# GpSimd sums half of the first layer's normalisation and mixes two tiles, and the key and value stores end in the next stage

## The reference, cut to what matters

```python
xn = layernorm(x)
# layer 0, attention: one head of width 128
q, k, v = split(xn @ Wqkv + bqkv);  a0 = softmax(q @ k.T * scale) @ v @ Wo + bo
# layer 0, second branch: 4 streams of 128 columns; 16 + 4 + 4 logits a row from the rms-normed xn
K = exp(H_res_logits / 0.1)                  # 4x4 for each row of x
for _ in range(50): row = 1 / (K @ col);  col = 1 / (K.T @ row)     # Sinkhorn, 100 halves
H_res = (1 - g) * I + g * row * K * col      # g = sigmoid(gate)
y = (streams weighted by H_pre) @ W_branch
f0 = H_res @ streams + H_post x y
x = x + a0 + f0
xn = layernorm(x)
# layer 1, attention: 32 query heads, 8 key heads, causal, keys and values by way of latents of 32
q = xn @ Wq.T;  k = (xn @ Wk_down.T) @ Wk_up.T;  v = (xn @ Wv_down.T) @ Wv_up.T
a1 = softmax(mask(q @ k.T * scale)) @ v @ Wo.T
# layer 1, second branch: one matrix product and 8 low-rank experts, 2 a row by a gate
f1 = xn @ weight.T + sum_e w_e * (xn @ A_e) @ B_e / 16
out = x + a1 + f1
```

## Time and profile before

| | |
|---|---|
| median of 3 runs | 2350.42 us (2345.44 to 2351.66) |
| the profiled execution | 2352.82 us, its span 2351.0 us |
| mean granted TensorE clock | 0.984 |
| PE, PEld busy | 2226.2 us (95%), 1810.6 us (77%) |
| DVE, ACT, POOL busy | 1536.4 us (65%), 1070.2 us (46%), 1014.8 us (43%) |

### The profile page before, as it was taken

One profiled execution on the slowest core, in us unless ns is written; L12 is line 12 of the kernel. 1 busy time (PEld: TensorE's weight loads), 2 busy tenths in 40 slices (PEclk: granted clock), 3 DMA queues, 4 the chain that ended last, 5 costly groups with the idle time before them and its releaser, 6 DMA issues. The chain is left out here.

```text
span 2351.0 us, 34663 instructions
## 1 busy us (share of the span) xinstructions
PE 2226.2 (95%) x11190; PEld 1810.6 (77%) x11190; DVE 1536.4 (65%) x3818; ACT 1070.2 (46%) x2279; POOL 1014.8 (43%) x1124
## 2 busy tenths in 40 slices
PE   6799897999999999999998888999999999999998
PEld 5554676888888888878786767888888888888886
DVE  6777565777677777756565564656566666666665
ACT  2456233545554444445444232545454544444444
POOL 5331713444445453676764011525344444434341
PEclk9999998999999999999999999999999999999999
DMA  9600564010101010111100464010101010101000
GB/s 349 207 0 10 213 234 156 10 63 9 63 9 63 14 58 27 45 47 42 44 28 6 173 245 157 28 48 24 62 9 62 9 62 9 62 9 62 27 32 32
DMA packets 74168, 165.26 MB, mean 70 GB/s; under 512 B 4721, under 2 KB 38897, under 8 KB 67442
## 3 DMA queue, kind: packets, MB, share of 16 engines
q1 hardware_dynamic: 73650, 162.95, 19.7%
q10 hardware_dynamic: 432, 1.32, 0.1%
HBM read 113.40 MB, written 72.61 MB: 79 GB/s over the span
## 5 line engine op out<-in xcount | busy, mean ns | idle before, releaser
L1852 DVE TENSOR_TENSOR pT<-psum,pT 128x512 fp32r<-128x512 f32 x576 | 387.1, 688 | 262.1 <-ACT pT L1900 259.8
L1752 POOL TENSOR_TENSOR probs_even<-probs_even,rinv 128x1024 f32<-128x1024 f32 (+2 forms) x192 | 241.0, 1255 | 553.9 <-DVE rinv L1843 553.9
L1900 ACT ACTIVATE pT<-psum 128x512 fp32r<-128x512 f32 x576 | 330.9, 596 | 317.8 <-PE psum L1961 317.7
L1838 DVE CUSTOM_DVE_ANT_0 psum<-psum,causal 128x256 f32<-128x256 f32 (+7 forms) x512 | 385.8, 766 | 37.3 <-PE psum L97 33.4
L1891 ACT ACTIVATE probs_even<-psum,nmax 128x1024 f32<-128x1024 f32 (+3 forms) x256 | 204.3, 798 | 247.2 <-DVE nmax L1838 243.4
L1752 POOL TENSOR_TENSOR probs_odd<-probs_odd,rinv 128x896 f32<-128x896 f32 (+2 forms) x192 | 198.9, 1043 | 257.5 <-DVE rinv L1843 257.3
L95 PE MATMUL psum<-keys,q 128*128 128x512 f32 (+3 forms) x768 | 265.7, 346 | 3.7 <-DVE q L1793 2.8
L97 PE MATMUL psum<-keys,q 128*128 128x512 f32 (+3 forms) x768 | 262.1, 341 | 0.0
L96 PE MATMUL psum<-keys,q 128*128 128x512 f32 (+3 forms) x768 | 262.0, 341 | 0.0
L95 PE MATMUL psum<-pT,vals 128*128 128x512 f32 x576 | 256.6, 445 | 4.3 <-DVE pT L1852 0.4
L1891 ACT ACTIVATE probs_odd<-psum,nmax 128x896 f32<-128x896 f32 (+3 forms) x256 | 176.4, 690 | 146.0 <-DVE nmax L1838 143.1
(11 more groups left out here) (304 smaller groups left out, 4423.5 us busy)
## 6 DMA issues: line engine op xcount, KB each, us to landing
k_parts<-kv_out SPq DMA_DIRECT2D x32, 512.0 KB, 4.7
wq<-wq_copy SPq DMA_DIRECT2D x16, 1024.0 KB, 4.8
v_parts<-kv_out SPq DMA_DIRECT2D x32, 512.0 KB, 3.6
wo<-wo_copy SPq DMA_DIRECT2D x16, 1024.0 KB, 4.8
keys<-k_parts SPq DMA_DIRECT2D x32, 512.0 KB, 4.5
vals<-v_parts SPq DMA_DIRECT2D x64, 256.0 KB, 3.1
acc<-in_x SPq DMA_DIRECT2D x4, 1024.0 KB, 12.0
xn_later<-xn SPq DMA_DIRECT2D x1, 2048.0 KB, 14.7
```

Source lines behind the costliest of these rows:

```text
L1752: pool.tensor_tensor(p, p, rinv[:, u, h:h + 1].to_broadcast([P, (TB - u) * P]), ALU.mult).then_inc(p_ok, 1)
L1838: dve.tensor_tensor_reduce(out=row, in0=row, in1=causal[:, S - n:S], scale=-1.0, scalar=-2 * MASKED, op0=ALU.add, op1=ALU.min, accum_out=n ...
L1852: dve.tensor_tensor(pT[:, n % PT_SLOTS, 1, :], bank[T_BANK + n % 2], f32(pT[:, n % PT_SLOTS, 0, :]), ALU.subtract).then_inc(t_lo, 1)
L1900: act.activation(pT[:, n % PT_SLOTS, 0, :], bank[T_BANK + n % 2], ACT.Copy).then_inc(t_hi, 1)
```

## The change

**Normalisation.** GpSimd, having scaled part 1 (`OWN`), also sums it by two additions: columns 2 and 3 onto 0 and 1 in place, then those two into `sk_s`. DVE sums part 0 alone and inverts both. The folding by logarithms stands at the stage's start, and the 68 halves run in one loop. The table of `between` has a maximum every 5 halves, 20 for a unit, and head sums at other places; the last unit's four head sums come after the mixing. **Attention of layer 0.** A unit's first scores are issued ahead of the head outputs of the unit before, the branch product stands between the second and third head output, and `share` takes one tile after each exponential. **Mixing.** DVE takes tiles 0 to 3, GpSimd 4 and 5 by `tensor_tensor` with broadcast weights (a product of 128x4x128 and an addition for each stream and for `y`), ScalarE and TensorE 6 and 7, with 8 slots at another place in memory and 4 of the 10 products issued within the last unit. GpSimd adds `bo` to tile 5 in `layer0_project`. **`layer1_inputs`.** With b = 0 too the main sums of tiles 6 and 7 stand after the `ups`; the weights' load and the spill or return stand ahead of the stores; the end of the stage no longer waits for the stores. That wait is in `layer1_attention`: SP's ahead of the keys, GpSimd's ahead of the mask. **`layer1_attention`.** Other `mixing_steps`.

```diff
+KV_SLOTS, UPS = 4, 32
...
-            add_bo(3)
-            add_bo(4)
+            for t in range(3, TB - 2):
+                add_bo(t)
...
-        FIRST_MAX, PER_UNIT = 3, 17
-        BY_ACT, SHARE_SLOTS = range(TB - 3, TB), UQ
-        CHUNKS = (SINKHORN_ITERS - SINKHORN_CHUNK - EARLY_HALVES // 2, SINKHORN_CHUNK)
+        FIRST_MAX, PER_UNIT, HALVES = 7, 20, 2 * SINKHORN_ITERS - EARLY_HALVES
+        BY_POOL, BY_ACT, SHARE_SLOTS = range(TB - 4, TB - 2), range(TB - 2, TB), 8
+        slots = placed(nc, "slots", XT, [P, SHARE_SLOTS, NS, D])
+        def out_bank(t):
+            return bank[(7, 6, 0, 1)[t % UQ] if t >= NT - UQ else 7 - t % 2][:]
...
-                with pool.Fori(0, count) as it:
-                    for half in range(2):
-                        for k in range(PARTS):
-                            factor = wide_rows(part_of(row, k)) if half else wide_cols(part_of(col, k))
-                            pool.wait_ge(factor_ok[k], it * 2 + (have + half))
-                            pool.tensor_tensor(part_of(T, k), part_of(K, k), factor, ALU.mult).then_inc(scaled[k], 1)
+            pool.wait_ge(k_ok, 1)
+            with pool.Fori(0, HALVES // 2) as it:
+                for half in range(2):
+                    for k in range(PARTS):
+                        factor = wide_rows(part_of(row, k)) if half else wide_cols(part_of(col, k))
+                        pool.wait_ge(factor_ok[k], it * 2 + (1 + half))
+                        pool.tensor_tensor(part_of(T, k), part_of(K, k), factor, ALU.mult).then_inc(scaled[k], 1)
+                    ours = turned_part(part_of(T, OWN)) if half else part_of(T, OWN)
+                    two = ours[:, :, :, 0:2]
+                    pool.wait_ge(scaled[OWN], it * 2 + (1 + half))
+                    pool.tensor_tensor(two, two, ours[:, :, :, 2:4], ALU.add).then_inc(halved, 1)
+                    pool.wait_ge(halved, it * 2 + (1 + half))
+                    pool.tensor_tensor(part_of(sm, OWN), two[:, :, :, 0], two[:, :, :, 1], ALU.add).then_inc(summed[OWN], 1)
+            pool.wait_ge(mix_ok, 1)
+            steps = 0
+            for t in BY_POOL:
+                x = x1[:, t, :].rearrange("p (i c) -> p i c", i=NS)
+                for j in range(NS + 1):
+                    stream = xn[:, t, j * D:(j + 1) * D] if j < NS else y[:, t, :]
+                    weight = T[:, t, :, j] if j < NS else rw[:, t, 1, :]
+                    if j == 0:
+                        pool.wait_ge(x1_ok, t + 1)
+                    if j == NS:
+                        pool.wait_ge(y_ok, t // UQ + 1)
+                    if steps:
+                        pool.wait_ge(blended, steps)
+                    pool.tensor_tensor(products[:], stream.unsqueeze(1).to_broadcast([P, NS, D]),
+                                       weight.unsqueeze(2).to_broadcast([P, NS, D]), ALU.mult).then_inc(blended, 1)
+                    pool.wait_ge(blended, steps + 1)
+                    pool.tensor_tensor(x, x, products[:], ALU.add).then_inc(blended, 1)
+                    steps += 2
...
-                dve.scalar_tensor_tensor(out=x1[:, t, :], in0=bank[7 - t % 2][:], scalar=rinv[:, t:t + 1], in1=x1[:, t, :],
+                dve.scalar_tensor_tensor(out=x1[:, t, :], in0=out_bank(t), scalar=rinv[:, t:t + 1], in1=x1[:, t, :],
                                          op0=ALU.mult, op1=ALU.add).then_inc(x1_ok, 1)
-            between = {0: [(weights_max, 0)], 2: [(weights, 0)], 5: [(gates, 0)], 9: [(later_head, 0)]}
-            for t in range(NT):
-                at = FIRST_MAX + PER_UNIT * (t // UQ)
-                k = t % UQ
-                between.setdefault(at + 4 * k, []).append((maximum, t))
-                between.setdefault(at + 4 * k + 3, []).append((invert, t))
-                between.setdefault(at + PER_UNIT + (14 if t // UQ < UNITS - 1 else 5) + k, []).append((add_heads, t))
+            between = {0: [(weights, 0)], 1: [(maximum, 2)], 3: [(maximum, 3)], 4: [(gates, 0)], 5: [(later_head, 0)],
+                       6: [(invert, t) for t in range(UQ)]}
+            for t in range(UQ, NT):
+                at = FIRST_MAX + PER_UNIT * (t // UQ - 1) + 5 * (t % UQ)
+                between.setdefault(at, []).append((maximum, t))
+                between.setdefault(min(at + 7, HALVES - 1), []).append((invert, t))
+            for t in range(NT - UQ):
+                between.setdefault(FIRST_MAX + PER_UNIT * (t // UQ + 1) + (1, 1, 3, 4)[t % UQ], []).append((add_heads, t))
+            weights_max(0)
+            dve.wait_ge(logs_ok, 2)
+            after(dve.tensor_tensor(Z[:], Z[:], wide_rows(lrow[:]), ALU.add))
+            dve.tensor_tensor(Z[:], Z[:], wide_cols(lcol[:]), ALU.add).then_inc(z_ok, 1)
             for k in range(PARTS):
-                dve.sem_inc(factor_ok[k], 1)
-            for part, count in enumerate(CHUNKS):
-                before = 2 * CHUNKS[0] * part
-                if part:
-                    dve.wait_ge(logs_ok, 2)
-                    after(dve.tensor_tensor(Z[:], Z[:], wide_rows(lrow[:]), ALU.add))
-                    dve.tensor_tensor(Z[:], Z[:], wide_cols(lcol[:]), ALU.add).then_inc(z_ok, 1)
-                    for k in range(PARTS):
-                        dve.memset(part_of(col, k), 1.0).then_inc(factor_ok[k], 1)
-                for half in range(before, before + 2 * count):
-                    for k in range(PARTS):
+                dve.memset(part_of(col, k), 1.0).then_inc(factor_ok[k], 1)
+            maximum(0)
+            maximum(1)
+            for half in range(HALVES):
+                for k in range(PARTS):
+                    if k != OWN:
                         by = turned_part(part_of(T, k)) if half % 2 else part_of(T, k)
                         dve.wait_ge(scaled[k], half + 1)
                         dve.tensor_reduce(part_of(sm, k), by, AX.X, ALU.add).then_inc(summed[k], 1)
-                        dve.wait_ge(summed[k], half + 1)
-                        dve.reciprocal(part_of(col if half % 2 else row, k), part_of(sm, k)).then_inc(factor_ok[k], 1)
-                    for step, t in between.pop(half, ()):
-                        step(t)
-                for k in range(PARTS):
-                    dve.wait_ge(factor_ok[k], before + part + 1 + 2 * count)
-                if part == 0:
-                    dve.sem_inc(factors, 1)
+                    dve.wait_ge(summed[k], half + 1)
+                    dve.reciprocal(part_of(col if half % 2 else row, k), part_of(sm, k)).then_inc(factor_ok[k], 1)
+                for step, t in between.pop(half, ()):
+                    step(t)
+            for k in range(PARTS):
+                dve.wait_ge(factor_ok[k], 1 + HALVES)
...
-            mixes, at = 0, 2 * sum(CHUNKS)
+            mixes, at = 0, HALVES
             ready = {t: (x1_ok, t + 1) for t in range(TB)}
-            for tiles in ((0, 1), (2, 3, 4)):
+            for tiles in ((0, 1), (2, 3)):
...
+            for t in range(NT - UQ, NT):
+                add_heads(t)
...
+            act.activation(lcol[:], col[:], ACT.Ln).then_inc(logs_ok, 1)
+            act.wait_ge(z_ok, 1)
+            act.activation(K[:], Z[:], ACT.Exp).then_inc(k_ok, 1)
+            act.wait_ge(chain, RW_MAX)
+            act.activation(rw[:], rw[:], ACT.Exp).then_inc(rw_exp, 1)
...
+            def share(t):
+                if t == 0:
+                    act.wait_ge(chain, RW_DONE)
+                if t >= UQ:
+                    act.wait_ge(xp_mm, t // UQ)
+                for j in range(NS):
+                    act.activation(shares[:, t % UQ, j, :], xn[:, t, j * D:(j + 1) * D], ACT.Copy,
+                                   scale=rw[:, t, 0, j:j + 1]).then_inc(xp_ok, 1)
...
+                    act.wait_ge(part_mm, e - SHARE_SLOTS + 1)
+                for i in range(NS):
+                    act.activation(slots[:, e % SHARE_SLOTS, i, :], xn[:, t, j * D:(j + 1) * D] if j < NS else y[:, t, :], ACT.Copy,
+                                   scale=T[:, t, i, j:j + 1] if j < NS else rw[:, t, 1, i:i + 1]).then_inc(part_ok, 1)
...
+                            if unit == UNITS and j % 2:
+                                product(j // 2)
...
-                        if t == 1:
-                            share(0)
-                        if t == 2:
+                        share(t)
+                        if t == UQ:
...
+                        if unit == 2:
+                            if qt == 0:
+                                act.wait_ge(m.ffn_in, 16 * 5)
+                            weight_high(wf_h[:, qt, :], wf_l[:, qt, :])
+                            if qt:
+                                high, low = m.right[0][qt - 1]
+                                weight_high(high[:], low[:])
...
-                if 0 < unit < UNITS:
-                    share(unit)
...
-            high, low = m.right[0][-1]
-            act.activation(high[:], f32(low[:]), ACT.Copy).then_inc(m.ffn_hi, 1)
+            for e in range(TB // 2, (NS + 1) * len(BY_ACT)):
```

(57 more changed lines are left out.)

79 lines of the change are left out of this document (17 added, 62 removed).

## The result

The changed kernel takes **2369.67 us** (median of 4 runs, 2369.08 to 2371.58) against 2350.43 us: 1.0079 times as long, with a 95% interval of 1.0064 to 1.0094. It is 19 us slower where 20 us less were forecast, and lies outside the range. The profiled execution has a span of 2367.3 us, 16.3 more than that of before.

A forecast was written before the change was run, and what follows sets the result against it. TensorE was taken to bound the attention stages, GpSimd and DVE's chain the normalisation, stores `layer1_inputs`. Terms +4 - 15 - 9 + 0 = -20 us from 2352.8 gave 2332.8, carried over to the median as 2330 us; range 2312 to 2346.

The forecast's parts named there:

- Mixing steps: First attention stage: GpSimd's steps move from units 5 and 6 to 2 and 7; net 0 us, between -6 and +7.
- The net of 0: Sum for the attention mixing steps: 7.7 us of `probs_even` waits gone, against 2.4 us delays in three iterations and 3.5 us key waits twice.
- GpSimd's sums: Second stage: GpSimd sums part 1, so a plain half takes 1.35 us, not 0.91; stretch to the weights 110.6 us, +3.
- DVE's wait of the earlier trace should go; I leave 2 us: Second stage: DVE's 8.3 us wait for scores goes with earlier scores and spread shares, leaving 2 us for units 2 and 3.
- Rival B: Second stage: GpSimd's sums are dear, 1.55 us a half, 13 us more, 2343 us; chance 0.14.
- Mixing: First layer, from the weights on: GpSimd's operations block DVE's steps; 46 us against 45.5, bounds 31 and 53.
- rival A: First-layer mixing: no blocking of DVE by GpSimd, tail 31 us, 15 us less, 2315 us; chance 0.18.
- `layer1_inputs`, b = 0: First half of the rows: earlier stores, loads ahead of them, no wait for the last landing; -15 us, bounds -8 and -17.
- Second half: Second input stage: loads ahead of stores give -6, half the bytes in the spill's return -3; -9 us, bounds -4 and -11.
- Rival C: Slower: a normalisation half costs 1.65 us and eats 20 us of gain; at 1.8 us the kernel takes 2360 us; chance 0.07.
- Rival D: Input stages: stores set everything anyway, so they give 5 + 3 us instead of 24; 2346 us; chance 0.09.

The follow-up runs named there:

- a2: The changed kernel, with SP issuing the third tile's loads behind those of keys, first values and output weights: 2352.7 us, ratio 1.0004.
- c1: The changed kernel, with ScalarE's copy of `oT` ahead of the last exponential of the next unit in the second stage: 2361.1 us, ratio 1.0056.
- a4: The changed kernel, with both parts of the normalisation summed by DVE, as before the change: 2356.2 us, ratio 1.0024.
- c2: b2 and c1 together: 2319.9 us, ratio 0.9874 against the kernel before.
- b3: The changed kernel, with the head sums of tiles 10 and 11 after 8 mixing steps instead of 12 and 16: 2365.1 us, ratio 1.0054.
- a3: The changed kernel without GpSimd's mixing in the first layer; DVE takes tiles 0 to 4: 2360.1 us, ratio 1.0038.
- b2: b1 with GpSimd's split of the query weights held until 8 keys products are stored, in both input stages: 2324.3 us, ratio 0.9874.
- b4: The changed kernel, with the wait for all stores back at the end of the input stages: 2372.8 us, ratio 1.0083.
- b1: The changed kernel with the alterations of a2, a3 and a4 together: 2332.9 us, ratio 0.9913.

## Why the prediction was wrong, step by step

**Mixing steps, the step that failed most.** The prediction saw that keys would be issued behind the third tile's load, about 10 us later, and put 3.5 us of waiting on it, twice. The mechanism was right and the size wrong: keys 13.1 and 9.7 us later, 5.9 us of waiting each time, and about 2 us of lower clock behind each (9 x 0.2), where 7 us in all were forecast. a2 takes 17.7 us away with SP's order alone. The term that was mis-sized both times is the landing. I took the 4.5 us of one transfer of keys; from the issue of the first transfer to TensorE's first product it was 7.2 and 7.1 us. There are two transfers, the second one landed 6.6 us after its issue (4.9 and 4.5 before), and the values, which were also overdue, are issued right behind them. For the second time these 2.6 us more are the whole miss. The first time keys were also 3.3 us later than forecast, but TensorE came 3.4 later itself (100.1 us behind the load of `wq`, 96.7 before). The lower clock had no term at all.

The net of 0 does not follow from its own terms either. They are -7.7 for the waits for `probs_even`, +7 for keys and three delays of 2.4 us, which is +6.5; the 0 leaves the delays out. They were there: in a2, without the waits for keys, the `probs_even` waits are gone but those for `probs_odd` are 10.2 us instead of 4.7, and all waits for probabilities, with the "issue" ones, are 14.0 us against 13.6 before. So with keys in time the new steps give nothing and cost nothing: 911.9 us in a2, 912.0 before.

A correction to "The kernel before": the three numbers of a unit in `mixing_steps` are not for iterations 5, 6 and 7. They stand for the unit's three scalings, alike in each of these iterations, and the steps follow the scaling. The third tile's load needs the 15th step, and by `7: (0, 0, 3)` that stands behind the third scaling of unit 7.

**GpSimd's sums.** 1.35 us a half forecast, 1.31 measured; a maximum adds 0.46 us to its half and the next together, 0.53 forecast. What failed is "DVE's wait of the earlier trace rows should go; I leave 2 us": it was 11.1 us, and 3.2 for head outputs, 12.3 more than forecast; all other terms together came out 4.6 below theirs. I let the longer halves cost their own length and nothing else. But they delay the maxima, the maxima ScalarE's exponentials, and behind the last of these stands the copy of `oT`, for which TensorE waits with a falling clock, and with it the next scores. c1 shows that chain: one instruction moved takes 5.7 us off the stretch. It is not the whole: with the short halves of a4 DVE waits 12.2 us for scores all the same, more than the 8.3 of before, and the stretch takes 107.6 us, as before. So the new order of this stage, which the forecast let pay for the sums, brought nothing by itself, and the sums cost 10.7 us on top. What those last waits hang on stays open; c2 shows that it is not the copy. Rival B had the place right (the stage slower than forecast), not the cause: a half was not dearer than priced.

**Mixing.** The blocking that the forecast took from the earlier trace rows is there: GpSimd's 20 operations take 25.1 us (26 forecast), DVE gets about one step past each, and rival A is out. The Trainium skill (SBUF — State Buffer, "Who interferes with whom") says that a VectorE instruction with two SBUF inputs contends with a GpSimd instruction that reads SBUF, and that the port pair which they share is an exclusive lock. The 1.26 us for a step beside GpSimd, against 0.265 alone, agree. The tail was 48.8 us, not 46, since the head sums that TensorE waits for stood between the blocked steps (b3: 3.8 us). The larger miss is what it was compared with. The forecast set mixing with GpSimd, blocked or not, against the 45.5 us of before; it never priced the rest of the edit (four products issued early, eight slots, the last head sums behind the mixing) without GpSimd. a3 has that at 39.8 us.

**`layer1_inputs`, b = 0: -15 forecast, -5.9 measured.** The forecast has three terms, and all fell short. Stores 5.4 us earlier: they came 1.4 earlier. ScalarE was 4.8 earlier, DVE was not, because the weights' earlier load also moved GpSimd's eight splitting operations to where DVE works with two inputs in SBUF. I had used the blocking for the mixing and overlooked it here; b2 shows it, 2.6 us to the first store and 3.3 behind it. Stores at full rate, 47 us from the first one to the last landing, 5.5 less than before: the first 17 us moved 291 GB/s, and keys went out 49.9 us behind the first store, 2.6 less than before. And the stage's end 4 us ahead of the last landing: it was 2.8 ahead, 1.9 of them reached the scores (12.9 us behind the issue of keys, 14.8 before), and b4 prices the moved wait at 3.0 us. That is 1.4 + 2.6 + 1.9 = 5.9. With the split held back, b2 has 128.9 us from the stage's start to scores where the kernel before has 142.3: 13.4 of the forecast 15. So GpSimd's split beside DVE's gate work makes 5.9 us (b2 against b1) of the 9.1 that this stage missed. The rows of the changed kernel's end of the stage:

```profile
370.28 1.28 DVE L1113 TENSOR_TENSOR acc<-acc,psum 128x512 f32<-128x512 f32 x2
...
374.37 0.81 SPq L1696 DMA_DIRECT2D keys<-k_parts  x2
```

DVE's last operation ends at 371.6, keys are issued at 374.4: the lead is 2.8 us.

**Second half: -9 forecast, -7.4 measured.** The long waits of ScalarE behind the weights' load are gone (longest for a slot of keys 2.0 us, 6.8 before), as forecast.

Rival C gave the sign and half of the loss (2360 us), by dear sums; it did not happen that way. Rival D gave the first half of the rows 5 us, close to the measured 5.9, but not for its reason, as b2's 13.4 shows; the second half gave 7.4 against its 3.

## What to carry to other kernels

Work moved to an engine that shares ports with the loaded one is paid for by that one; price it against leaving the work where it was, and look for every other place where the move makes the two meet, also by an earlier load that only releases the helper sooner. When a chain gets longer, follow each result that it delays to the engine that waits last, and look at what stands behind the waiting instruction in that engine's list. In a queue that issues in order, a transfer that waits for slow work has to stand behind those that the bounding engine needs next; here two moved lines are worth 17 us.

## What the runs showed of the hardware

DVE's 128x256 multiplication with two inputs in SBUF took 0.42, 0.69, 0.95, 1.11 or 1.45 us by where it fell against GpSimd's operations of 1.0 to 1.4 us, while reductions with one input between them stayed at 0.42 and head sums with one input in PSUM at 0.70 to 0.75. The best version here, c2, takes 2319.9 us, 28 less than the kernel before on the same chips (ratio 0.9874).
